# Expert layer at the end of a two-layer kernel: a second set of four PSUM banks, own banks for each down product, and expert weights summed by a tree of additions

## The reference

```python
x0 = x[:, :ROUTE_LEN].reshape(b, -1)
logits = x0 @ switch_w.T + switch_b
probs = jax.nn.softmax(logits, axis=-1)
gate, top_idx = jax.lax.top_k(probs, TOPK)
xh = x.reshape(b, s, H, DH).transpose(0, 2, 1, 3)
w1s, b1s = (w1[top_idx], b1[top_idx])
w2s, b2s = (w2[top_idx], b2[top_idx])
h = jnp.einsum('bhsd,bkfd->bkhsf', xh, w1s) + b1s[:, :, None, None, :]
h = jax.nn.gelu(h, approximate=False)
o = jnp.einsum('bkhsf,bkdf->bkhsd', h, w2s) + b2s[:, :, None, None, :]
o = (o * gate[:, :, None, None, None]).sum(axis=1)
o = o.transpose(0, 2, 1, 3).reshape(b, s, d)
out = x + o
return out @ w3.T + b3
```

## Time and profile before

| | us |
|---|---|
| median of 3 runs (1122.37 to 1125.25) | 1123.57 |
| the profiled execution, its own time | 1119.19 |
| its span in the trace | 1117.4 |
| span: PE busy / DVE busy / ACT busy | 1052.7 / 697.5 / 553.6 |

### The profile page before, as it was taken

The page is one execution under the profiler, slowest core; times in us unless marked ns, Lnnn a source line. Parts: engine busy times, 40 slices in busy tenths (PEclk is TensorE's granted clock), DMA queues, the critical chain, the costliest instruction groups (busy, mean ns, idle before and its releaser), DMA issues.

```text
span 1117.4 us, 26010 instructions
## 1 busy us (share of the span) xinstructions
PE 1052.7 (94%) x10262; PEld 759.8 (68%) x10262; DVE 697.5 (62%) x2080; ACT 553.6 (50%) x1427; POOL 435.0 (39%) x391
## 2 busy tenths in 40 slices
PE   5988999999999999999999899999999999999977
PEld 2747788888887855573648567766767676767545
DVE  5218889889989942313133675846584767576853
ACT  2437777887877743212132544445454535443430
POOL 1022203303523711100004574857474657678510
PEclk8579999999999999999999899999999999999989
DMA  9300000000000003700003001200130003002002
GB/s 341 121 1 1 2 1 0 0 0 0 0 2 1 2 1 69 258 1 1 1 0 77 20 20 38 59 20 20 26 71 21 20 21 77 21 20 77 21 2 77
DMA packets 24207, 42.19 MB, mean 38 GB/s; under 512 B 6576, under 2 KB 14768, under 8 KB 22704
## 3 DMA queue, kind: packets, MB, share of 16 engines
q1 hardware_dynamic: 24112, 40.87, 12.3%
HBM read 21.98 MB, written 2.10 MB: 22 GB/s over the span
## 4 chain that ended last, share of the span: by engine, by line
PE 51%; DVE 5%; ACT 2%; issue 1%; POOL 0%; DVEq 0%; ACTq 0%
PE quad L1946 9%; PE quad L1597 7%; PE bank L1988 7%; PE quad L2008 7%; PE bank L1991 5%; PE bank L1890 5%; PE quad L2019 5%; PE quad L1954 1%; ACT act_probs L2242 1%; DVE act_probs L2342 1%; ACT act_probs L2249 1%; PE quad L2083 1%; PE bank L2083 1%; PE bank L1909 1%; DVE wq_wo L2356 1%
## 5 line engine op out<-in xcount | busy, mean ns | idle before, releaser
L2585 POOL TENSOR_TENSOR act_probs<-act_probs,rden 128x512 f32<-128x512 f32 (+3 forms) x128 | 171.2, 1341 | 155.8 <-DVE rden L2361 155.7
L2242 ACT ACTIVATE act_probs<-act_probs,neg_max 128x256 f32<-128x256 f32 (+3 forms) x256 | 140.8, 552 | 82.6 <-DVE neg_max L2342 82.3
L1946 PEld LDWEIGHTS quad<-hT,ug_queries 128*128 128x128 f32 x1024 | 120.5, 194 | 30.6 <-issue 18.6
L1946 PE MATMUL quad<-hT,ug_queries 128*128 128x128 f32 x1024 | 132.2, 283 | 3.0 <-ACT act_probs L2249 2.2
L2342 DVE CUSTOM_DVE_ANT_0 act_probs<-bank,mask 128x256 f32<-128x256 f32 (+3 forms) x256 | 114.9, 486 | 6.6 <-PE bank L1991 6.1
L1597 PE MATMUL quad<-hT,ug_raw_switch 128*128 128x512 f32 x256 | 115.8, 603 | 0.0
L1988 PE MATMUL bank<-ckvT,ug_raw_switch 64*128 64x512 f32 (+3 forms) x512 | 105.8, 480 | 6.9 <-DVE neg_max L2342 6.9
L2361 DVE RECIPROCAL rden<-den 128x2 f32<-128x2 f32 x128 | 20.6, 161 | 121.0 <-ACT act_probs L2242 120.9
L1612 DVE SCALAR_TENSOR_TENSOR act_probs<-quad,ws_up,silu_keys 128x512 f32<-128x512 f32 x32 | 24.0, 750 | 102.4 <-ACT silu_keys L1607 102.4
L1597 PEld LDWEIGHTS quad<-hT,ug_raw_switch 128*128 128x128 f32 x256 | 48.0, 192 | 55.7 <-issue 55.0
L1607 ACT ACTIVATE silu_keys<-quad,ws_gate 128x512 f32<-128x512 f32 x32 | 22.0, 688 | 120.5 <-PE quad L1597 120.5
(11 more groups left out here) (384 smaller groups left out, 2419.7 us busy)
## 6 DMA issues: line engine op xcount, KB each, us to landing
rope_swapped<-gate SPq DMA_DIRECT2D x120, 64.0 KB, 2.0
wmod<-in_wmod SPq DMA_DIRECT2D x2, 1536.0 KB, 9.5
x_pairs<-in_x SPq DMA_DIRECT2D x2, 1024.0 KB, 9.6
x_rows<-x_pairs SPq DMA_DIRECT2D x8, 256.0 KB, 4.8
wq_wo<-in_wq_nopeT SPq DMA_DIRECT2D x1, 2048.0 KB, 8.5
wq_wo<-in_wo SPq DMA_DIRECT2D x1, 2048.0 KB, 12.5
down_raw_out<-x_pairs SPq DMA_DIRECT2D x16, 128.0 KB, 2.4
ug_queries<-in_switch_w SPq DMA_DIRECT2D x1, 2048.0 KB, 7.6
```

The source lines that it names most:

```text
L1946: mm = nc.tensor.matmul(out[:, P * i:P * i + P], w[:, kt, HP * half + i, :], k.hT[:, kt, b, cols], start=(kt == 0), stop=(kt == KT - 1))
L2242: nc.scalar.activation(tile, tile, ACT.Exp, bias=neg_max[:, r, e:e + 1], scale=-1.0, accum_out=den[:, r, e:e + 1])\
L2585: nc.gpsimd.tensor_tensor(tile, tile, rden[:, t % RING, :].unsqueeze(2).to_broadcast([P, 2, cols]), ALU.mult)\
```

## The change

Banks 4 to 7 become one tensor too, `quad2`. Up products of odd groups go there, so PE waits for the gelus of two groups before (`g - 2`) in place of one. Down products of kt = 0 go to banks 0 to 3, those of kt = 1 to banks 4 to 7, each after the gelus that read these banks. The late tile's turn and ACT's modulation of it move behind all four groups. The last attention projection goes to bank 5, and its ACT copy is cut in two halves of heads. In `route_picks` the reduction becomes three additions of 4, 2 and 1 experts' widths. `down_latest` moves between the first and the second `last_product`, the first `add_rows` behind the LATEST rows on DVE, and the third early logits on DVE ahead of the sums of a norm group.

```diff
-    SHIFTED, BIASED = 3, 22
+    SHIFTED, BIASED = 3, 24
...
     def filled(*what):
+        if what == ("out", NB - 1):
+            return bank[5]
         return bank[banks.bank(*what)]
...
             def project_out(n, part):
                 out = filled("out", n)
                 if part == 0:
-                    clear(banks.previous("out", n))
+                    if n < NB - 1:
+                        clear(banks.previous("out", n))
                     pe.wait_ge(s["oT_taken"], n + 1)
+                elif n == NB - 1:
+                    pe.wait_ge(s["oT_taken"], NB + 1)
...
             def up_experts(g):
                 kt, c = divmod(g, 2)
+                if g == 1:
+                    wait_taken(pe, "out", NB - 1)
                 for h in range(2):
-                    if g >= 1:
-                        pe.wait_ge(gelu_done, 2 * (g - 1) + h + 1)
+                    if g >= 2:
+                        pe.wait_ge(gelu_done, 2 * (g - 2) + h + 1)
                     for b in range(B):
                         for r in range(2 * h, 2 * h + 2):
                             rows = slice(ROW * r, ROW * r + ROW)
-                            mm = nc.tensor.matmul(bank[r][ROW * b:ROW * b + ROW, EARLY], bd[0][rows, c, b].rearrange("p s f -> p (s f)"),
+                            mm = nc.tensor.matmul(bank[4 * (g % 2) + r][ROW * b:ROW * b + ROW, EARLY], bd[0][rows, c, b].rearrange("p s f -> p (s f)"),
                                                   k.hT[rows, kt, b, EARLY], start=True, stop=True)
                     mm.then_inc(up_made, 1)
 
             def up_latest():
-                pe.wait_ge(gelu_done, 4 * KT)
+                pe.wait_ge(z_made, B)
...
             def down_experts(kt):
                 for c in range(2):
-                    pe.wait_ge(gelu_done, 4 * kt + 2 * c + 2)
-                    if kt == 1 and c == 0:
-                        pe.wait_ge(z_made, B)
+                    pe.wait_ge(gelu_done, 2 * KT + 2 + 2 * kt)
                     for r in range(R):
                         for b in range(B):
                             rows = slice(ROW * b, ROW * b + ROW)
-                            mm = nc.tensor.matmul(bank[4 + b][ROW * r:ROW * r + ROW, EARLY], bd[1][rows, c, b].rearrange("p s f -> p (s f)"),
+                            mm = nc.tensor.matmul(bank[4 * kt + b][ROW * r:ROW * r + ROW, EARLY], bd[1][rows, c, b].rearrange("p s f -> p (s f)"),
                                                   gel[rows, kt, c, r, EARLY], start=(c == 0), stop=(c == 1))
                 mm.then_inc(expert_made, 1)
...
-            wait_taken(pe, "out", NB - 1)
             pe.wait_ge(blocks_made, 1)
-            for g in range(3):
+            for g in range(2 * KT):
                 up_experts(g)
+            pe.wait_ge(blocks_made, 2)
+            down_experts(0)
+            pe.wait_ge(gelu_done, 4 * KT)
             for kt in range(KT):
                 norms.turn(pe, LAST + 2, kt, bank[4 + kt])
-            up_experts(3)
-            pe.wait_ge(blocks_made, 2)
             pe.wait_ge(norms.taken, norms.done(LAST + 2, 1))
-            down_experts(0)
+            down_experts(1)
             up_latest()
-            down_experts(1)
             pe.wait_ge(pool_step, W3_GATED)
             pe.wait_ge(z_made, 2 * B)
-            for b in LAST_ORDER[0:2]:
-                last_product(b, (0, 1, 3))
+            last_product(LAST_ORDER[0], (0, 1, 3))
             down_latest()
+            last_product(LAST_ORDER[1], (0, 1, 3))
...
             for g in range(2 * KT):
                 kt, c = divmod(g, 2)
-                if g == 3:
-                    modulate_side(LAST + 2, 4)
                 for h in range(2):
                     act.wait_ge(up_made, 2 * g + h + 1)
-                    nc.scalar.activation(gel[:, kt, c, 2 * h:2 * h + 2, EARLY], k.quad[:, 2 * h:2 * h + 2, EARLY], ACT.Gelu, bias=bias1[:, c:c + 1])\
+                    nc.scalar.activation(gel[:, kt, c, 2 * h:2 * h + 2, EARLY], (k.quad, k.quad2)[g % 2][:, 2 * h:2 * h + 2, EARLY], ACT.Gelu, bias=bias1[:, c:c + 1])\
                         .then_inc(gelu_done, 1)
+            modulate_side(LAST + 2, 4)
             act.wait_ge(up_made, 4 * KT + 1)
...
-                after(nc.vector.tensor_reduce(pick[w], prod[w].rearrange("p n e f -> p n f e"), AX_X, ALU.add))
+
+            def picks_summed(w):
+                for n in (E // 2, E // 4):
+                    after(nc.vector.tensor_tensor(prod[w][:, :, 0:n], prod[w][:, :, 0:n], prod[w][:, :, n:2 * n], ALU.add))
+                after(nc.vector.tensor_tensor(pick[w], prod[w][:, :, 0], prod[w][:, :, 1], ALU.add))
...
                 if t == SLOTS + 1:
+                    early_logits(2)
                     dve.wait_ge(s["added"], NB - 1)
                     norms.sums(dve, LAST + 1)
-                    early_logits(2)
...
                 dve.wait_ge(expert_made, kt + 1)
                 for b in range(B):
-                    nc.vector.scalar_tensor_tensor(zT[:, kt, b, EARLY], bank[4 + b][:, EARLY], bsum[:, b:b + 1], k.hT[:, kt, b, EARLY],
+                    nc.vector.scalar_tensor_tensor(zT[:, kt, b, EARLY], bank[4 * kt + b][:, EARLY], bsum[:, b:b + 1], k.hT[:, kt, b, EARLY],
                                                    ALU.add, ALU.add).then_inc(z_made, 1)
-            add_rows(0)
...
-            for m in range(1, 2 * B):
+            for m in range(2 * B):
                 add_rows(m)
```

More of the change, by code:

```diff
@@ L2248, in take_out @@
                     wait_made(act, "out", n - 1)
-                nc.scalar.activation(oT[:].rearrange("p n (i c) -> p n i c", c=BLK),
-                                     av.rearrange("p i (n c) -> p n i c", c=BLK), ACT.Copy).then_inc(s["oT_taken"], 1)
+                to, src = oT[:].rearrange("p n (i c) -> p n i c", c=BLK), av.rearrange("p i (n c) -> p n i c", c=BLK)
+                for heads in [slice(0, NP)] if n < NB - 1 else [slice(0, HP), slice(HP, NP)]:
+                    nc.scalar.activation(to[:, heads], src[:, heads], ACT.Copy).then_inc(s["oT_taken"], 1)
             modulate_side(LN0B + 1)
@@ L2425, in route_ranks, with picks_masked, picks_placed, route_picks @@
                 after(nc.vector.tensor_tensor(hot_g[:], hot[:], spread(prob[:], [P, 2, B, E], 1), ALU.mult))
-            def route_picks(w, hots):
+            def picks_masked(w, hots):
                 after(nc.vector.tensor_tensor(prod[w], spread(w12[w][:], [P, CB, E, FH], 1), spread(cb(hots), [P, CB, E, FH], 3), ALU.mult))
-                after(nc.vector.tensor_reduce(pick[w], prod[w].rearrange("p n e f -> p n f e"), AX_X, ALU.add))
+            def picks_summed(w):
+                for n in (E // 2, E // 4):
+                    after(nc.vector.tensor_tensor(prod[w][:, :, 0:n], prod[w][:, :, 0:n], prod[w][:, :, n:2 * n], ALU.add))
+                after(nc.vector.tensor_tensor(pick[w], prod[w][:, :, 0], prod[w][:, :, 1], ALU.add))
+            def picks_placed(w):
                 nc.vector.tensor_tensor(bd[w].rearrange("p c b s f -> p (c b) s f"), spread(pick[w], [P, CB, S2, FH], 2),
                                         parity[:].unsqueeze(1).unsqueeze(3).to_broadcast([P, CB, S2, FH]), ALU.mult).then_inc(blocks_made, 1)
+            def route_picks(w, hots):
+                picks_masked(w, hots)
+                picks_summed(w)
+                picks_placed(w)
             def route_biases():
@@ L2712, in build @@
         k.quad = stack.enter_context(nc.psum_tensor("quad", [P, 4, 512], F32))
-        k.bank = [k.quad[:, i] for i in range(4)] + [stack.enter_context(nc.psum_tensor(f"bank{i}", [P, 512], F32)) for i in range(4, 8)]
+        k.quad2 = stack.enter_context(nc.psum_tensor("quad2", [P, 4, 512], F32))
+        k.bank = [x[:, i] for x in (k.quad, k.quad2) for i in range(4)]
         allocate_residents(k)
```

## The result

| | before | changed |
|---|---|---|
| median of 4 executions, us | 1123.63 (1122.37 to 1125.25) | 1107.11 (1104.17 to 1109.65) |
| ratio, 95% interval | | 0.9851 [0.9824, 0.9879] |
| profiled execution, own time / span | 1119.19 / 1117.4 | 1106.67 / 1104.9 |

A forecast was written before the change was run, and what follows sets the result against it. Bound: a tail chain of PE, ACT and DVE waiting on each other. Down product 1 6.55 us earlier (front's 2.3 included) plus 1.65 for LATEST order made 8.2: 1123.57 to 1115.4 us; range 1114.2 to 1116.6, with rivals 1 and 2 1113.6 to 1118.6.

The forecast's parts named there:

- Front 2.3 us: Start of the up products: first gelus begin at 1075.15 instead of 1077.48, 2.3 us earlier.
- The tree: Routing picks on DVE: three additions take 1.47 us for a reduction of 1.87, saving 0.40 each time.
- The order of the LATEST products: Dense layer: LATEST down products between the first two dense products remove a wait for DVE, 1.65 us.
- Rival 2: Up products: the second set of banks gives nothing, PE and ACT alternating at 2.6 us; 1116.9 us, chance 0.10.
- The early logits: Third early logits on DVE, moved ahead of a norm group's sums: net nothing, between +0.1 and -0.1 us.
- the price of a down product: Each down product, from PE's start to DVE's: 2.72 us at full clock, 3.6 at half.
- my 8.2: Whole tail: the last dense wait's end at 1105.19 moves to 1097.0, 8.2 us earlier.
- the turn of the late tile: Between the down products: turn 0.45 us and ACT's modulation 0.80, 1.25 us now on the path.
- carried over to it, 1123.57 - 8.2: Final step: the gain summed on one profiled execution applied to the median before, giving 1115.4 us.
- rival 1: TensorE's clock in the tail falls all the same: gain 5.5 to 7.2, some 6.4 us, 1117.2; chance 0.27.
- rival 4: Dense layer: sparser start leaves the clock at half; with all 64 instructions 7.2 us slower, 1130.8; chance 0.02.

The follow-up runs named there:

- a1_no_tree: Changed kernel with the reduction in place of the three additions, for both weights: mean 1109.6 us, ratio 0.9896 to the kernel before, tail 48.29 us.
- a4_latest_last: Changed kernel with the LATEST down products behind both first dense products again: mean 1109.3 us, ratio 0.9887 to the kernel before, tail 49.53 us.
- a6_one_set_filled: Changed kernel with up products in one set of banks and idle matmuls in PE's waits: mean 1111.8 us, ratio 0.9933 to the kernel before, tail 50.41.
- a3_shared_down: Changed kernel with the second down product waiting for DVE's rows of the first: mean 1110.8 us, ratio 0.9897 to the kernel before, tail 49.97 us.
- b3_shifted: Kernel before with 64 already satisfied waits on TensorE ahead of its wait for the attention's last output: mean 1120.5 us, ratio 0.9993, tail 61.17 us.
- b2_filled: Kernel before with idle matmuls in PE's waits around the up groups: mean 1118.0 us, ratio 0.9972, tail 54.83 us, all at full clock.
- a0_again: Changed kernel, unchanged, run for more executions: mean 1108.8 us, ratio 0.9909 to the kernel before, tail 47.61 us.
- b1_two_quads: Kernel before with only banks 4 to 7 declared as one tensor: mean 1121.7 us, ratio 0.9997, tail 62.98 us.
- a5_filled: Changed kernel with three idle matmuls ahead of the first up group and one behind it: mean 1109.5 us, ratio 0.9907 to the kernel before, tail 47.46.
- b0_again: Kernel before, unchanged, run again: mean 1123.2 us, ratio 1.0012, tail 58.12 us.

## Why the prediction was wrong

*What held.* The chain and its releases were as said. Front 2.3 us: gelus and first down product came within 0.1 us of the forecast. The tree, 0.40 twice, 0.83 measured (a1_no_tree). The order of the LATEST products, 1.65: 1.75 measured (a4_latest_last). Rival 2 fell: the second set is worth 2.4 to 3.0 us by its order alone (a6_one_set_filled). The Trainium skill, TensorE: Matmul & The Clock Gate, section "HAM oscillation", says of a matmul kernel that PSUM double-buffering gave no further gain; that doesn't carry over to this one, where PE waited for ACT at each group. Each of these sizes comes from taking one step back alone; a3_shared_down adds 1.2 us for the down products' own banks. Together they make 6.2 to 6.8 of the 7 us that the schedule gave. The first up group's start without the attention's last output was not tested alone. The early logits brought nothing, as said: the turned rows came 0.1 us later, seen from the transpose (1058.55 - 1054.85 = 3.70, before 1060.89 - 1057.32 = 3.57).

*A term mis-sized: the price of a down product.* I took 2.72 us for the full clock and 3.6 for the half, from two rows. Both held something foreign. The first held a pause of 0.75 us that belongs to a place in the instruction stream (b3_shifted, b2_filled). The second product began at 1085.18 us while the last up group still ran:

```profile
1083.90 2.04 PE L2040 MATMUL quad<-hT,ug_raw_switch 32*32 32x384 f32 x32
```

That this overlap made it longer is argued, not tested. By itself a product takes 1.96 us to DVE at the full clock (changed kernel) and 3.25 at the half (a3_shared_down). In the changed kernel the pause lies in the LATEST up products, beside DVE's rows, which end at about the same time: the 0.63 us there cost next to nothing, the 0.79 of a0_again some 0.1. Twice 0.76 is 1.5 of the 1.8 us that the tail gained beyond my 8.2. The rest is small: the turn of the late tile began 0.1 us before DVE and was 0.36 and not 0.45 ahead of its modulation, and from the start of the dense layer to the end of the tail it was 16.8 us and not 17.0.

*The step that failed: "carried over to it, 1123.57 - 8.2".* I made the sum against one profiled execution and moved it to the median, as if every execution of the old kernel lost as much to the clock in its tail as that one. I put the difference at nothing, without a reason. The profile of before has 10 us at half clock in the tail, which cost 2.7. Two others of what is the same program, but for a declaration (b1_two_quads) or for satisfied waits (b3_shifted), have 24 and 21, and tails of 63.0 and 61.2 us. I weighed the clock only as something that the new kernel might lose (rival 1), and as a danger of its dense layer (rival 4). Both mechanisms were real, but it was the old kernel that paid them, and the change took them away with the waits.

The sizes: the four profiles of the old program have a mean tail of 59.9 us, 5.1 above the filled one and 12.5 above the changed kernel's. By the means of all executions it is 13.0 in all; 7.4 for the schedule at equal, full clock (54.83 to 47.46) leaves 5.6 for the clock, of which the profile that I forecast on held 2.7 (7.4 and 2.7 are the 10.0 between the two profiles' tails). The mean clocks (0.9674 and 0.9756) make about 73 and 54 us at half, 19 less. At 0.26 us lost for each such microsecond (2.7 for 10, before) or 0.34 (8.2 for 24, b1_two_quads) that is 5 to 6.5. So the three ways agree as far as four tails and a mean clock of the whole program can show it. Of the 13.0, then, 8.2 is my sum, 1.8 the mis-sized term, and 3.0 what the average old execution lost to the clock beyond the profiled one. The range of the prediction ended at a gain of 10.0.

*The rest of the 16.5*, 3.5 us, is luck: few executions on each side, in a program whose single executions spread over 11 us. The clock also differs between executions ahead of the tail, most often in the program's first 110 us. The windows of 60 to 110 us, before and changed, lie in the same early stage, which the change doesn't touch, and differ:

```profile
60.00:110.00 50.00, 43.29 (x399) 31.65 (x399) 26.17 (x84) 29.48 (x63) 14.85 (x23) 0.85 0.01 1
```

```profile
60.00:110.00 50.00, 43.13 (x428) 32.14 (x427) 28.37 (x94) 31.91 (x74) 14.83 (x23) 0.92 0.00 1
```

The changed kernel got through 29 more matmul instructions in the same 50 us (x428 and x399), at a granted clock of 0.92 and not 0.85. That is the 2.5 us ahead of the tail in the two profiles. Kernels of both kinds have both sorts of start: a5_filled, with the changed kernel's tail, ran 1112.0 us in its profiled execution, 5.3 more than the changed kernel's, all ahead of the tail. What sets the clock there I didn't test.

## What to carry to other kernels

Where TensorE waits in short steps, its clock can be part of the price of a wait: 1.2 us of added waiting cost 2.5 in a3_shared_down. One profile shows one draw of the clock, so look at the mean clock of every execution before carrying a difference from a profile to a median, and fill the waits once with idle matmuls to learn how much of a stage is clock and how much is schedule. Check in the trace that the clock is full and that no real product waits behind an idle one. And before taking a duration from a row, look at the weight loads inside it for a pause that does not belong to the operation.

## What the runs showed of the hardware

In a3_shared_down PE ran a down product of 1.92 us and the late tile's turn at full clock and then idled for 2.01 us; the granted clock fell to half as the next product began. The tail of the old program spent 10 us at half clock in two profiles, 24 with only a declaration changed and 21 with 64 satisfied waits. A product of 64 instructions in 32x32 tiles takes 1.92 us at full and 3.2 at half clock. With idle matmuls in PE's waits the clock stayed full in the profiled tail (b2_filled), at a cost of up to 0.3 us where one of them ran into a real product's start. And a pause in PE's weight loads keeps its place in the instruction stream, 18 loads sooner for 36 instructions more. It was 0.54 us (a1_no_tree) to 1.28 us long (b0_again), and 0.75 and 1.28 in two profiles of one program; it was missing in two traces, and what it costs depends on the work beside it.
